# Scan pass of a four-layer network: PE spreads units 5, 9, 13, 17, 21 of a span, the stores of y leave on SP's queue, and the copies of C are made in three lots

## What is computed

```python
def step(state, inp):
    d, b, c, uu = inp
    dA = jnp.exp(d[..., None] * A_neg[:, None, :, :])
    state = dA * state + (d * uu)[..., None] * b[:, :, None, :]
    y = jnp.einsum('kbcn,kbn->kbc', state, c)
    return (state, y)
_, ys = jax.lax.scan(step, init, (d_t, B_t, C_t, u_t))   # 3136 steps
```

## Time and profile before

| | us |
|---|---|
| median of 3 runs (16746.03 to 16751.82) | 16748.27 |
| the profiled execution's own time | 16740.79 |
| its span, first to last instruction | 16739.1 |
| scans of layer 2, first start to last start | 8542.4 to 15092.7 |
| DVE busy with the scans (2688) | 5400.7 |
| POOL busy with b(n) (2688) | 5560.1 |
| PE busy over the whole span | 13258.6 (79%) |
| ACT busy over the whole span | 8476.8 (51%) |

### The profile page before, as it was taken

One profiled execution on the slowest core, in us unless ns is written; L12 is line 12 of the kernel. 1 busy time (PEld: TensorE's weight loads), 2 busy tenths in 40 slices (PEclk: granted clock), 3 DMA queues, 4 the chain that ended last, 5 costly groups with the idle time before them and its releaser, 6 DMA issues. The chain is left out here.

```text
span 16739.1 us, 371849 instructions
## 1 busy us (share of the span) xinstructions
PE 13258.6 (79%) x130080; PEld 8791.3 (53%) x130080; DVE 11153.8 (67%) x10439; ACT 8476.8 (51%) x15113; POOL 6761.1 (40%) x3199
## 2 busy tenths in 40 slices
PE   7889999899988965444657887888778878887799
PEld 5666666666666642221235555555455545554477
DVE  5666666666666655554568887888788878885532
ACT  4444444444444435445556666666666666662200
POOL 1000000000000003234368888888888888881100
PEclk9999999999999988776768888888888888886799
DMA  5222222222222226668599999999999998997611
GB/s 128 58 68 57 57 60 55 61 60 56 58 65 61 55 86 159 157 163 201 147 210 208 207 208 206 206 208 208 206 207 208 207 205 207 208 209 211 184 44 37
DMA packets 1861415, 2344.84 MB, mean 140 GB/s; under 512 B 1067492, under 2 KB 1757932, under 8 KB 1836012
## 3 DMA queue, kind: packets, MB, share of 16 engines
q1 hardware_dynamic: 1606124, 2120.92, 53.4%
q10 hardware_dynamic: 242816, 134.91, 4.0%
q0 software_dynamic: 12288, 86.71, 2.3%
HBM read 1814.60 MB, written 556.32 MB: 142 GB/s over the span
## 5 line engine op out<-in xcount | busy, mean ns | idle before, releaser
L1789 DVE TENSOR_TENSOR_SCAN L2.h<-L2.ps,L2.db 128x912 f32<-128x912 f32 x2688 | 5400.7, 2046 | 1181.3 <-ACT L2.db L1712 1068.1
L1601 POOL TENSOR_TENSOR L2.db<-L2.du,L2.bt 128x896 f32<-128x896 f32 x2688 | 5560.1, 2097 | 1068.7 <-ACT L2.du L1719 832.6
L1623 PE MATMUL L2.ps<-L2.dm,L2.wa 32*128 32x112 f32 x21504 | 2441.9, 326 | 503.4 <-DVE L2.h L1789 383.7
L1705 ACT ACTIVATE L2.ps<-L2.ps 128x896 f32<-128x896 f32 x2688 | 2440.9, 908 | 492.0 <-PE L2.ps L1623 440.3
L1645 PE MATMUL L2.ps<-L2.h,L2.cd 128*8 128x96 f32 x50176 | 2576.8, 362 | 79.9 <-ACT L2.ysum L1726 67.1
L1623 PEld LDWEIGHTS L2.ps<-L2.dm,L2.wa 32*128 32x128 f32 x21504 | 1898.5, 220 | 1306.4 <-DVE L2.h L1789 785.6
L1635 PE MATMUL L2.ps<-L2.few,L2.fan 8*128 8x448 f32 x2688 | 1603.3, 680 | 832.9 <-ACT L2.du L1719 826.7
L1645 PEld LDWEIGHTS L2.ps<-L2.h,L2.cd 128*8 128x8 f32 x50176 | 1435.6, 108 | 806.3 <-ACT L2.ysum L1726 236.1
L1726 ACT COPY L2.ysum<-L2.ps 128x384 f32<-128x384 f32 x1568 | 751.7, 479 | 771.1 <-PE L2.ps L1645 666.5
L314 POOL TENSOR_TENSOR L1.x_res<-L1.x_res,L1.ob 96x3136 f32 (+1 forms) x16 | 95.4, 5977 | 2583.9 <-ACT L1.qv L457 2583.9
L1635 PEld LDWEIGHTS L2.ps<-L2.few,L2.fan 8*128 8x128 f32 x2688 | 443.5, 205 | 1192.4 <-ACT L2.du L1719 861.7
(11 more groups left out here) (258 smaller groups left out, 21196.1 us busy)
## 6 DMA issues: line engine op xcount, KB each, us to landing
L2.du<-du SPq DMA_DIRECT2D x4032, 224.0 KB, 6.0
L2.dm<-d SPq DMA_DIRECT2D x896, 336.0 KB, 7.2
y<-L2.ysum ACTq DMA_DIRECT2D x896, 84.0 KB
L0.left<-table SPq DMA_DIRECT2D x48, 1176.0 KB
L0.right<-table SPq DMA_DIRECT2D x48, 1176.0 KB
L1.left<-table SPq DMA_DIRECT2D x48, 1176.0 KB
L1.right<-table SPq DMA_DIRECT2D x48, 1176.0 KB
du<-L2p.work SPq DMA_DIRECT2D x64, 784.0 KB, 7.8
```

The lines of the kernel that those rows point to most:

```text
L1601: pool.tensor_tensor(db[:, n % RB, :, 2:ROW], du[:, n % RD, :].rearrange("p (c t) -> p c t", t=SPAN), row, ALU.mult)\
L1623: mm = pe.matmul(decays[n % RA][:, lo:lo + SPAN], wa[rows, u * QUAD + e, :], dm[rows, u * QUAD + e, :], start=True, stop=True)
L1705: act.activation(a, a, ACT.Exp).then_inc(a_ready, 1)
L1789: dve.tensor_tensor_scan(h[:, half, u * UNIT:(u + 1) * UNIT, :].rearrange("p c t -> p (c t)"), decays[n % RA], db[:, n % RB, :, :].rearran ...
```

## The change

PE now spreads units 5, 9, 13, 17 and 21 (five a span). `few` i is for unit 4i+5 and not 4i+3, while the fans and copies stay at the same units of PE and ACT; those at n = 20 to 22 fall away. SP therefore loads 19 units a span, not 18. The four stores of a half are issued by SP, two at step 5 and two behind the du load of step 6, in the half-span after the one in which the sums were taken; the last ones follow SP's loop. ACT makes C's copies in lots of 3, 3 and 2 behind its units 11, 12 and 13. The diff, with the adaptation of counts for the odd number of fans left in:

```diff
-            return n % 4 == 3
-        FANS = 2 * UNITS // 4
+            return n > 1 and n % 4 == 1
+        FANS = 2 * UNITS // 4 - 1
...
             def load_few(k, s, i):
-                before = count(sp, k, s, 2 * FANS, 2 * (i - 1))
-                n = 4 * i + 3
+                before = count(sp, k, s, 2 * FANS, 2 * max(i - 1, 0))
+                n = 4 * i + 5
...
+            def store_y(k, s, half, quarters):
+                for q in quarters:
+                    at = s * SPAN + SPAN // 4 * q
+                    if k % 2:
+                        at = at * -1 + (TOK - SPAN // 4)
+                    rows = slice(at, at + SPAN // 4) if isinstance(s, int) else bass.ds(at, SPAN // 4)
+                    place = y_dram[k, :, rows, half * HALF:(half + 1) * HALF]
+                    sp.dma_start(place, ysum[32 * q:32 * q + BATCH, :, :]).then_inc(y_stored[half], 16)
+
-            def half_span(k, s, half, later, table):
+            def half_span(k, s, half, earlier, later, table):
+                fills = count(sp, k, s, 2 * FILLS, (half - 1) * FILLS)
...
-                    if n % 4 == 0:
+                    if n % 4 == 0 and n // 4 < FANS:
                         load_few(k, s, n // 4)
...
+                    if 5 <= u <= 6 and earlier is not None:
+                        if u == 5:
+                            sp.wait_ge(sum_out, fills + 2)
+                            steady(sp)
+                        store_y(*earlier, half, range(2 * (u - 5), 2 * (u - 5) + 2))
...
             for half in range(2):
+                sp.wait_ge(sum_out, (DIRS * HALVES - 1 + half) * FILLS + 2)
+                store_y(DIRS - 1, NSPANS - 1, half, range(4))
...
-                            pool.wait_ge(du_copied, copies + 2 * (n // 4 + 1))
+                            pool.wait_ge(du_copied, copies + 2 * (n // 4))
...
-                    if n % 4 < 2:
+                    if n % 4 < 2 and n // 4 < FANS:
                         fan_out(n // 4, n % 4, k, s)
...
-            def make_cd(k, s, fills):
-                act.wait_ge(cc_in, count(act, k, s, 16, 16))
-                act.wait_ge(sum_ready, fills + 2 * FILLS)
-                for b in range(BATCH):
+            def make_cd(k, s, fills, batches):
+                if batches[0] == 0:
+                    act.wait_ge(cc_in, count(act, k, s, 16, 16))
+                    act.wait_ge(sum_ready, fills + FILLS)
+                for b in batches:
...
             def copy_du(i, g, units, copies):
-                n = 4 * i + 3
+                n = 4 * i + 5
...
-                    if 1 <= n % 4 <= 2:
+                    if 1 <= n % 4 <= 2 and n // 4 < FANS:
                         copy_du(n // 4, n % 4 - 1, units, copies)
                     decay(n, spreads)
                     carry(half, u, units, begun)
-                if not first:
-                    act.wait_ge(sum_out, before + (FILLS + 2))
-                    steady(act)
-                    if half:
-                        store_y(k, s, 0)
-                    elif begun:
-                        store_y(k - 1, NSPANS - 1, 1)
-                    else:
-                        store_y(k, act.snap(s - 1), 1)
-                if half == 0:
-                    make_cd(k, s, before)
+                    if UNITS - 1 <= n <= UNITS + 1:
+                        at = 3 * (n - UNITS + 1)
+                        make_cd(k, s, count(act, k, s, 2 * FILLS), range(at, min(at + 3, BATCH)))
```

More of the change, by code:

```diff
@@ L1562, in span @@
                     later = (k, s + 1) if isinstance(s, int) else (k, sp.snap(s + 1))
-                half_span(k, s, 0, (k, s), k if k and isinstance(s, int) and s == 0 else None)
-                half_span(k, s, 1, later, k + 1 if last and k + 1 < DIRS else None)
+                if isinstance(s, int) and s == 0:
+                    earlier = (k - 1, NSPANS - 1) if k else None
+                else:
+                    earlier = (k, s - 1) if isinstance(s, int) else (k, sp.snap(s - 1))
+                half_span(k, s, 0, earlier, (k, s), k if k and isinstance(s, int) and s == 0 else None)
+                half_span(k, s, 1, earlier, later, k + 1 if last and k + 1 < DIRS else None)
             sp.wait_ge(cleared, 1)
@@ L1578, in _ @@
                 span(k, NSPANS - 1, True)
+            for half in range(2):
+                sp.wait_ge(sum_out, (DIRS * HALVES - 1 + half) * FILLS + 2)
+                store_y(DIRS - 1, NSPANS - 1, half, range(4))
             for half in range(2):
@@ L1631, in fan_out @@
                 if g == 0:
-                    pe.wait_ge(few_in[i % 2], count(pe, k, s, 16 * FANS // 2, 16 * (i // 2 + 1)))
+                    pe.wait_ge(few_in[i % 2], count(pe, k, s, 16 * len(range(i % 2, FANS, 2)), 16 * (i // 2 + 1)))
                 if not (isinstance(copies, int) and copies == 0):
@@ L1767, in _ @@
                 take_sum(DIRS - 1, 1, f, (DIRS * HALVES - 1) * FILLS)
-            act.wait_ge(sum_out, DIRS * HALVES * FILLS + 2)
-            store_y(DIRS - 1, NSPANS - 1, 1)
         @block.vector
```

## The result

The change makes the kernel slower: 17079.83 us (median of 4 runs, 17064.64 to 17087.08) against 16749.89 us, ratio 1.0196, 95% interval 1.0178 to 1.0214. The profiled execution took 17078.11 us, its span 17076.4.

The account below looks back on a forecast made before the run. ACT's order was taken to hold DVE and POOL at 58.5 us a span; after the change loads 46.0 plus stores 2 x 7.8 give 61.6, (61.6 - 58.5) x 112 = +347 us: 17095 us median, range 16400 to 17500.

Parts of the forecast that it names:

- serial stores: Likeliest case, chance 0.60: on SP's queue loads stand behind stores, 61.6 us a span, range 58.8 to 65.2.
- What bounds the kernel before: Scan pass, 58.5 us a span: no engine full, ACT's order holds DVE and POOL; POOL idles 8.5 before PE-spread units.
- C in lots: ACT's copies of C, 2.34 us spread over three units with time to spare: zero for the lots.
- Stores on SP's queue: Deciding term: four stores take 7.8 us from the loads, bounds 4.3 and 8.4; 46.0 + 2 x 7.8 = 61.6 a span.
- the packets' own time: Four stores' cost to the loads by their packets, an estimate of 5.2 us between bounds 4.3 and 8.4.
- ACT's new wait: Rival, chance 0.12: take 0 waits for SP's stores, decays and PE's lots behind it; loop of 58.8 us a span, 16780.
- All hidden: Rival, chance 0.06: only the engines count in the scan pass, 51.4 us a span, 15950 us.
- The signs: Right: POOL waits for du loads, some 10 us a span, landing well above 6.0. Wrong: landing stays about 6.

Follow-up runs that it names:

- Two buffers: Kernel after the change with two buffers ysum, one for each half, so take 0 waits for stores issued a half-span earlier: 16561.81 us.
- The best: Kernel after the change with two buffers ysum, stores one each on ACT's queue, and units 3, 7, .. 23 spread by PE again: 16280.26 us.

## Why the prediction was right, and where it was not

The forecast was 17095 us, slower, and 17080 was measured. The number is right and the likeliest case behind it is not: that serial stores were priced at 61.6 us a span and the loop through ACT's wait turned out at 61.4 is luck.

- **What bounds the kernel before** held in part: POOL's idle of 8.5 us a span before its PE-spread units went (768.0 us of waits for copies to none). But that it was the copies' *place* fell. C in lots alone took 1.4 us a span off, and in the two kernels with two buffers the old places cost nothing.
- **C in lots** was priced as a move that costs nothing; its gain was not given a size of its own. It was 159 us, the only part that was a gain on the kernel before.
- **Stores on SP's queue**, the term that decides in the prediction, was mis-sized. I took 7.8 us of load time per four stores, the row of the group alone on its queue. Two buffers give 4.3 to 5.4; the packets' own time of 5.2 stood between the bounds and was passed over. Even at 5.4 the loads need 56.9 us, under today's 58.5: this term alone would have made the kernel faster. The choice "by the nearest row" mistook the time a queue needs for the time it takes from its neighbours. The stretch of 10.2 us above, in which the loads moved 1.45 MB beside the stores, shows it in the kernel itself: at 258 GB/s that is worth 5.6 us, so the four stores took 4.6, an estimate from this one half.
- **ACT's new wait**, a rival with chance 0.12, is what happened. Its 58.8 us is 2.6 short. Means over all halves whose take 0 lies between 9000 and 15000 us say where, first and second halves in turn. Lots 1 to 5 take 12.0 and 9.8 us, where 10.3 and 9.5 were put down: PE's clock comes back later, and of the 2.7 us that the half shown has above 10.3, 2.4 are its two lots with fans at clock 0.50. From the end of b(11) or b(23) to the first issue it is 2.5 and 4.1 us, where 2.7 was put down (B, a quarter of delta and the backlog); in the second half SP has the load of `few` still to issue, which waits for a fan. First issue to take 0 is 10.6 and 10.5, where 9.0 and the two loads' 1.8 stood. With the other steps the loop measures 31.3 + 30.3 = 61.6 us in this stretch, which is the whole period.
- **The Trainium skill's rule** that DMAs of all issuing engines run and interleave on the same DMA engines ("DMA: Bandwidth & Descriptors", "Issuing engines are not separate DMA queues") would have kept the stores' cost at about today's 4.5 us. The 4.3 to 5.4 us in SP's queue agree with that, and the 1.8 us a span that the kernel with two buffers gains with its stores on ACT's queue say that it holds only nearly, if the gain is not SP's own time.
- **All hidden**, 51.4 us, was not reached by any kernel. The best has 54.3, and POOL's largest wait in it is for loads.
- **The signs** told the two apart. Du's time to landing should have risen well above 6.0 and fell to 5.5, which the prediction itself had named as a sign of being wrong. POOL's waits for loads should have been some 10 us a span and were 2, and the loads at a store phase moved more than today, not less. ACT's wait in front of take 0 was there, but both cases had it.

## What to carry to other kernels

Moving a DMA off a busy engine moves its issue and also its landing: look for who waits for the landing, and whether that waiter is upstream of the next issue. If it is, the two form a loop whose length is the period, and a second buffer can be worth more than a rearrangement of the queue (here 518 us against 84). A case and its rival can give nearly the same number; name beforehand the wait that only one of them has.

## What was not expected of the hardware

- Four stores of 84 KB in ACT's queue took 8.4 us alone and about as long beside loads; but in the kernel with stores back on ACT, at a DMA share of 1.10, take 0 waited 13.33 us for them. A queue of its own is no right of way here.
- PE's clock comes back later behind a wait. It is at 0.50 ahead of take 0 in both kernels. Before, it is at 1.00 from lot 1 on; after, with PE busy for 2.15 of the 6 us of the wait, it stayed at 0.50 through the next 11 us in which PE was busy again, and a fan lot took 4.1 instead of 2.91 us. The 32 matmuls of a lot take 1.64 us at either level; what gets longer are the fan and the spread (0.65 to 1.1 us). So a stall costs more than its length, some 2.0 us a span here (lots 1 to 5 of both halves).
- A period bound by waiting had its DMA engines at 0.67 in two of the four stretches shown, though the share over the whole pass, 0.87, looks nearly full.
